# First self attention of a two-layer decoder: the order of TensorE's work inside a wave

## The reference, cut to what matters

```
scores = einsum('bhqd,bhkd->bhqk', q, k) * scale
mask = (i[None, :] > i[:, None]) | (i[:, None] - i[None, :] >= WINDOW)
scores = where(mask, -inf, scores)
combined = concatenate([scores, sink_col], axis=-1)
probs = softmax(combined, axis=-1)[..., :-1]
out = einsum('bhqk,bhkd->bhqd', probs, v)
out = out.transpose(0, 2, 1, 3).reshape(Bq, Tq, H * D)
return out @ Wo + bo
```

## Time and profile before

| | us |
|---|---|
| median of 3 runs | 1651.32 (1651.06 to 1651.63) |
| span of the profiled execution, from its first to its last instruction | 1651.2 |
| TensorE matmul busy | 1590.1 (96%) |
| VectorE busy | 942.8 (57%) |
| ScalarE busy | 731.2 (44%) |
| GpSimd busy | 665.9 (40%) |

### The profile page before, as it was taken

The page is one execution under the profiler, slowest core; times in us unless marked ns, Lnnn a source line. Parts: engine busy times, 40 slices in busy tenths (PEclk is TensorE's granted clock), DMA queues, the critical chain, the costliest instruction groups (busy, mean ns, idle before and its releaser), DMA issues.

```text
span 1651.2 us, 24551 instructions
## 1 busy us (share of the span) xinstructions
PE 1590.1 (96%) x9832; PEld 1353.0 (82%) x9832; DVE 942.8 (57%) x1535; ACT 731.2 (44%) x1227; POOL 665.9 (40%) x483
## 2 busy tenths in 40 slices
PE   7999999989999999989999989998989999999998
PEld 7898666878899998768889976887668888888887
DVE  6555664366545455677768566354766455554554
ACT  3113655322587765666511156332635334353342
POOL 3875542441498873421137633212512422222321
PEclk9999999999999999999999999999999999999999
DMA  4110003123222007200001100110001111111111
GB/s 166 52 65 28 2 2 116 56 84 127 95 89 65 14 1 267 93 1 1 1 13 65 51 27 1 50 39 32 21 23 43 45 64 46 51 46 51 51 58 45
DMA packets 28580, 88.52 MB, mean 54 GB/s; under 512 B 4154, under 2 KB 4282, under 8 KB 28215
## 3 DMA queue, kind: packets, MB, share of 16 engines
q1 hardware_dynamic: 28468, 86.96, 15.4%
HBM read 85.11 MB, written 1.84 MB: 53 GB/s over the span
## 4 chain that ended last, share of the span: by engine, by line
PE 83%; DVE 8%; ACT 5%; issue 3%; POOL 1%; ACTq 0%; DVEq 0%; POOLq 0%
PE PS L261 19%; PE PS L263 18%; PE PS L262 18%; PE PS L266 7%; PE PS L1125 4%; PE PS L1462 3%; PE PS L1477 2%; PE PS L561 2%; PE PS L952 1%; PE PS L585 1%; PE PS L1709 1%; PE PS L1697 1%; PE PS L551 1%; DVE sm L1731 1%; PE PS L569 1%
## 5 line engine op out<-in xcount | busy, mean ns | idle before, releaser
L307 POOL TENSOR_TENSOR HL<-stg,HL 128x1024 fp32r<-128x1024 f32 (+2 forms) x111 | 243.8, 2199 | 543.5 <-ACT HL L302 525.5
L261 PE MATMUL PS<-XT,HL 128*128 128x448 f32 x608 | 225.0, 370 | 4.3 <-DVE XT L342 3.7
L263 PE MATMUL PS<-XT,HL 128*128 128x448 f32 x608 | 223.1, 367 | 0.0
L262 PE MATMUL PS<-XT,HL 128*128 128x448 f32 x608 | 223.1, 367 | 0.0
L302 ACT ACTIVATE HL<-stg 128x1024 fp32r<-128x1024 f32 (+2 forms) x111 | 104.5, 944 | 216.6 <-PE PS L263 200.9
L261 PE MATMUL PS<-HL,XT 128*128 128x512 f32 (+1 forms) x380 | 137.8, 363 | 2.2 <-DVE XT L1981 1.4
L263 PE MATMUL PS<-HL,XT 128*128 128x512 f32 (+1 forms) x380 | 134.8, 355 | 0.0
L262 PE MATMUL PS<-HL,XT 128*128 128x512 f32 (+1 forms) x380 | 134.8, 355 | 0.0
L261 PEld LDWEIGHTS PS<-XT,HL 128*128 128x128 f32 x608 | 115.0, 189 | 16.6 <-DVE XT L342 4.9
L262 PEld LDWEIGHTS PS<-XT,HL 128*128 128x128 f32 x608 | 115.1, 189 | 9.2
L263 PEld LDWEIGHTS PS<-XT,HL 128*128 128x128 f32 x608 | 114.9, 189 | 9.2
(11 more groups left out here) (299 smaller groups left out, 3813.7 us busy)
## 6 DMA issues: line engine op xcount, KB each, us to landing
stg<-in_wst SPq DMA_DIRECT2D x87, 512.0 KB, 3.2
stg<-in_wst SPq DMA_DIRECT2D x16, 352.0 KB, 3.0
stg<-in_wst SPq DMA_DIRECT2D x16, 320.0 KB, 3.2
wsum<-in_wfc SPq DMA_DIRECT2D x8, 512.0 KB, 3.7
wsum<-in_wpj SPq DMA_DIRECT2D x8, 512.0 KB, 3.5
raw<-in_wfc SPq DMA_DIRECT2D x8, 512.0 KB, 7.5
stg<-in_wst SPq DMA_DIRECT2D x16, 256.0 KB, 2.6
raw<-in_wpj SPq DMA_DIRECT2D x7, 512.0 KB, 7.0
```

The lines of the kernel that those rows point to most:

```text
L261: e.matmul(out, lh, rh, start=start, stop=False)
L262: e.matmul(out, lh, rl, start=False, stop=False)
L263: return e.matmul(out, ll, rh, start=False, stop=stop)
L307: e.tensor_tensor(slot(k)[:, 1, 0:n], stg[k % NSTG][:, 0:n], slot(k)[:, 0, 0:n].bitcast(F), A.subtract).then_inc(*done("pool_w", k))
```

## The change

It moves calls in `pe_att0` alone, in the loop over the waves. No instruction is added or removed, no wait is written anew, and the lists of the other engines stay.

```
                 if w > 1:
                     turn(2 * w - 3)
-                    values(2 * w - 4)
                 if w < W0:
                     less(2 * w)
+                    less(2 * w + 1)
                 if 0 < w <= W0:
                     turn(2 * w - 2)
-                if w < W0:
-                    less(2 * w + 1)
                 if w > 1:
+                    values(2 * w - 4)
                     values(2 * w - 3)
```

## The result

| | before | after |
|---|---|---|
| median, us (runs) | 1651.47 (4, 1651.06 to 1652.89) | 1685.63 (4, 1685.04 to 1687.81) |
| span of the profiled execution, us | 1651.2 | 1683.6 |

The changed kernel is slower by the ratio 1.0209 (95% interval 1.0196 to 1.0222; it is not exactly the quotient of the medians), 34.2 us between the medians. Forecast were 1684.4 in 1680 to 1690, so that the time, the sign and the size came out. Of the cause, two parts need telling apart: what a wave costs, and what happened in the tail.

What follows compares the result with a forecast made beforehand. TensorE bounds the waves before, at 7.40 us; the change closes a 9.57 us ring. Wave 15's values come 31.85 later, the tail adds 1.26: 33.1 on the 1651.2 span is 1684.3, median 1684.4, range 1680 to 1690.

Steps and rivals of the forecast that it cites:

- The ring: Each wave: values, copy out, exponentials, masks, scores, maxima, second subtraction, turn, values again; 9.57 us against 7.40, chance 0.85.
- Rival A: ScalarE's copy does not hold the exponentials, only the maxima hold TensorE: wave 8.53 us, time 1667, chance 0.04.
- The maxima stand bare: TensorE waits uncovered for VectorE's maxima: about 0.4 us ahead of the first subtraction, about 0.55 ahead of the second.
- links: The start-to-start steps of a wave, each taken from a profile row, known to some 0.05 us, summing to 9.57.
- the rounding: L302 between the exponentials of waves 2 and 3 counts 0.95 us each, 1.90 together, where most fell in slack.
- The start: From the stage's first mask matmul to the values of wave 2: 22.37 us, against 19.84 before.
- The tail: From the values of wave 15 to the last turn: 10.30 us against 9.04 before, 1.26 more.
- rival C: TensorE's clock falls: 1757 if for the whole stage, 1690 for about a wave; chance beyond one wave 0.07.
- Its buffer is free: The second turn's buffer is free 2.00 us after the first turn starts; that turn comes 2.9 after, so stays hidden.
- The sign for rival C: PEclk below 1 in the window 160:290 would show the clock falling and the forecast wrong.
- Rival B: The four subtraction matmuls standing together save TensorE time, with wave 2's mask wait 3.3 us: 1648, chance 0.02.
- the hold: ScalarE's copy out(2w-4) waits for the moved value group, and both exponentials of the wave queue behind it.

Runs made afterwards that it cites:

- e1: Changed kernel with ScalarE's copy out(2w-4) put behind both exponentials in waves 2 to 15: 1666.82 us, ratio 1.0090.
- e4: Kernel before with both value groups at the wave's end, and ScalarE's copy out(2w-4) behind both exponentials: 1662.04 us, ratio 1.0060.
- e3: Kernel before with both value groups together at the wave's end, subtractions where they were: 1683.42 us, ratio 1.0190.
- e5: Kernel before with only ScalarE's list altered, copy out(2w-4) behind both exponentials: 1653.35 us, ratio 1.0001.
- e6: Changed kernel with the row maximum taken over 57 of the 113 columns of a head: 1678.08 us, ratio 1.0150.
- e7: Kernel before with the row maximum taken over 57 of the 113 columns of a head: 1653.18 us, ratio 1.0000.
- e9: Changed kernel with the rounding of waves 2 and 3 (L302) moved behind the second exponential: 1684.74 us, ratio 1.0195.
- e8: Changed kernel with idle mask matmuls in TensorE's gaps of waves 16 and 17: 1686.83 us, ratio 1.0204.
- e10: Changed kernel with the rounding of waves 2 and 3 behind the second exponential, plus idle mask matmuls in waves 16 and 17: 1682.24 us, ratio 1.0181.
- e2: Kernel before with the two subtractions together, value groups where they were: 1654.16 us, ratio 1.0010.

## Why the prediction was right

- *The ring closes over ScalarE's copy.* Shown by e1, and by e4 against e3, both 1.19 us a wave, with e5 as the control. Rival A had the trace as e1 makes it (8.53 forecast, 8.31 measured), and its price, 1667, is e1's time. It was not what the change did.
- *The maxima stand bare on the ring.* Shown by e6 and e7. By starts the second subtraction of the changed kernel waits 207.17 - (206.16 + 0.48) = 0.53 us and the second mask pair 202.24 - (201.43 + 0.45) = 0.36, as forecast; the idle that the profile prints for them, 0.37 and 0.16, is shorter, since it counts the modelled end of the matmul before as busy.
- *The size of a wave.* 9.57 forecast, 9.50 measured. The turn takes 0.86 ahead of the values and not 0.91; the other links agree to 0.02. Over 13 waves that is 0.9 too much. The two waves with the rounding came out at 10.45, and e9 puts the 0.95 where the forecast had it.
- *The start* was 22.37 for 22.31: the wave of 7.89 us between the score products of waves 1 and 2, with the second exponential right behind the first, was right.
- *The tail was mis-sized.* "In all 10.30, 1.26 more" of the forecast is 12.94, 3.90 more. Of this, 2.31 is the clock's fall, rival C on a small scale, which the forecast had only as a bound of the range; e8 and e10, with the clock whole, show 10.63 both times. The last 0.33 is in the links. From a copy's end to the turn that waits for it the forecast took the 0.05 of an exponential and a mask matmul, three times; the trace has 0.14, and it stood so in the kernel before, where the last turn starts at 264.32:

```profile
263.28 0.90 ACT L623 ACTIVATE PT<-PS 112x896 f32<-112x896 f32 x1
```

That is 0.27 of it. From the copy out to the o_hi copy it is 0.57 and not 0.44 (292.20 to 292.77 in e10, 294.97 to 295.54 in the changed kernel), and small differences of the other sign take 0.07 back.
- *Part of the closeness is luck.* The misses of -0.9 and +2.6 leave the stage 1.7 us longer than worked out (160.64 against 158.98). The profiled execution does not show it only because its stage began 1.65 us earlier, for a reason ahead of the change; so the last turn came at 297.44, where "near 297.4" was forecast. A further 1.8 us lie outside the sum: the profiled execution of the changed kernel is listed at 1685.43 with a span of 1683.6, so "the median is 0.1 above" the span does not carry from one kernel to the other.
- *Covered needs.* "Its buffer is free" was right for the changed kernel; the copy was over at 206.8, 0.85 us ahead of the turn. The same need was overlooked in e3 and e4, and each was off by 0.3 a wave for it.
- *The sign for rival C* came up: "if PEclk in 160:290 is below 1". The window prints 0.99, by the fall at its end; from 160 to 285 it is 1.00. Taken by its words the sign would have named the wrong rival, since the clock costs 2.3 us of the stage's 34.8 and the ring nearly all the rest. The window should have ended ahead of the tail.
- *Rival B* (faster by standing together) is not what happened: e2, with the hold out of play, has a wave of 7.56 for 7.39 and a ratio of 1.0010 (1.0000 to 1.0020). As the forecast said, the second maximum comes too late for it.

None of these kernels is faster than the one before beyond its interval.

## What to carry to other kernels

Moving a group later in one engine's list moves everything that waits for it, in every other list that was not moved: before a reorder, find for each moved group its consumer and read what stands behind that consumer in the consumer's own list. If the way leads back to the engine that was reordered, add up the ring's links; the longer of the ring and the engine's own work is the wave. A need that is covered today (a copy out of a buffer, a maximum) should be written down with the group that covers it, since it turns bare when that group goes.

## What the runs showed of the hardware

- The clock fell in some executions and not in others at the same waves. Waves 3 and 4 kept 1.00 in the changed kernel; in e8, with the same instructions there, windows of them had 0.67 and 0.66, at a price of 1.57 and 1.02 us. Otherwise waves of 9.50 us, with TensorE busy for 84%, kept 1.00 in the four profiles of that order (after, e8, e9, e10), and e10 kept it in the tail also. In e6 it fell to 0.50 from 175 to 180 us. In the tail the changed kernel and e9 have the same wait of 2.42 us ahead of the first turn; the turn behind it took 1.71 us in the one and 0.95 in the other, where the next turn was the first of 1.72.
- Like matmuls on end are cheaper than the same ones alone. One value group of four matmuls takes 0.90 us to the next group; two on end take 211.10 - 209.45 = 1.65 in e1, so four more add 0.75, 188 ns each. The starts lie 0.43, 0.37, 0.38 and 0.47 us apart for each two of the eight (209.45, 209.88, 210.25, 210.63, and the mask at 211.10), so the extra is at both ends of the row, where kinds change. The Trainium skill (TensorE: Matmul & The Clock Gate, Back-to-back issue gap) gives the gap of a single matmul as columns divided by 2.4 plus 2.5 ns, here 189 ns; the run agrees inside a row of like matmuls, and not at its ends. The forecast, which took the rows' 0.90, was right for a group by itself.
